# New instruction orders for all five engines of a transformer-layer kernel, and other places for its filler matmuls

## The reference

```python
h = x @ tok_W + position_table                       # (8, 1024, 128)
z = layernorm(h)
q, k, v = z @ Wq + bq, z @ Wk + bk, z @ Wv + bv      # 8 heads of 16
p = softmax((q @ k.T + causal_mask) / 4)             # 1024 x 1024 for each head
h = h + (p @ v) @ Wo + bo
z2 = layernorm(layernorm(h)) * ln_scale + ln_bias
shared = swiglu(z2 @ shared_in.T) @ shared_out.T + b # 256 hidden
hid    = swiglu(z2 @ expert_in.T)                    # 256 hidden, one for all experts
# one of 2 groups by argmax, 2 of its 4 experts by softmax, weights comb (S, 8)
h = h + shared + counts @ expert_bias + sum_e comb[:, e] * (hid @ expert_out[e].T)
```

## Time and profile before

| | |
|---|---|
| median of 3 runs | 1005.61 us (1005.56 to 1009.05) |
| the profiled execution | 1005.95 us, of which 1004.2 us is the span from the first to the last instruction |
| PE busy | 929.9 us, 93% of the span |
| DVE, ACT, POOL busy | 809.5, 595.0, 375.5 us |
| mean granted PE clock | 0.973 of full |

### The profile page before, as it was taken

One profiled execution on the slowest core, in us unless ns is written; L12 is line 12 of the kernel. 1 busy time (PEld: TensorE's weight loads), 2 busy tenths in 40 slices (PEclk: granted clock), 3 DMA queues, 4 the chain that ended last, 5 costly groups with the idle time before them and its releaser, 6 DMA issues.

```text
span 1004.2 us, 17715 instructions
## 1 busy us (share of the span) xinstructions
PE 929.9 (93%) x5672; PEld 548.5 (55%) x5672; DVE 809.5 (81%) x2529; ACT 595.0 (59%) x1365; POOL 375.5 (37%) x526
## 2 busy tenths in 40 slices
PE   6688999999999999999998999999999999999986
PEld 6653454456655646456644656347554655444464
DVE  5688897898779888897979898798978987795363
ACT  4015547665756675756764665666576666666743
POOL 6404322424345243433534253343434152422433
PEclk8789899999989999999999999999999999999999
DMA  4221010200010111110111101110101000100000
GB/s 139 69 67 52 14 33 15 67 30 2 31 59 30 38 31 34 45 48 1 44 35 36 37 17 36 45 54 13 44 20 59 31 12 33 44 2 1 11 11 12
DMA packets 45981, 35.21 MB, mean 35 GB/s; under 512 B 10816, under 2 KB 44608, under 8 KB 45760
## 3 DMA queue, kind: packets, MB, share of 16 engines
q1 hardware_dynamic: 43680, 31.97, 9.8%
q10 hardware_dynamic: 2208, 2.10, 0.6%
HBM read 4.28 MB, written 4.19 MB: 8 GB/s over the span
## 4 chain that ended last, share of the span: by engine, by line
PE 33%; DVE 12%; ACT 3%; issue 3%; POOL 2%; SPq 1%; DMA 1%; ACTq 0%; POOLq 0%; DVEq 0%
PE bank_w L589 5%; PE bank_p L571 5%; PE bank_s L541 4%; PE bank_f L674 3%; PE bank_f L676 3%; PE bank_f L675 3%; DVE mx_far L772 2%; DVE bank_s L776 2%; PE bank_f L475 2%; PE bank_m L640 1%; PE bank_f L477 1%; PE bank_f L476 1%; ACT pt L1043 1%; PE bank_m L604 1%; PE bank_m L614 1%
## 5 line engine op out<-in xcount | busy, mean ns | idle before, releaser
L1043 ACT ACTIVATE pt<-bank_p 128x512 f32<-128x512 f32 (+3 forms) x768 | 342.0, 491 | 188.3 <-PE bank_p L571 158.3
L776 DVE CUSTOM_DVE_ANT_0 bank_s<-bank_s,causal 128x384 f32<-128x384 f32 (+3 forms) x512 | 242.9, 507 | 43.7 <-PE bank_s L541 41.8
L541 PE MATMUL bank_s<-k_stack,q_stack 96*128 96x512 bf16 (+3 forms) x768 | 222.0, 336 | 19.7 <-DVE mx L776 10.5
L571 PE MATMUL bank_p<-q_stack,k_stack 99*128 99x512 bf16 (+3 forms) x768 | 213.3, 334 | 11.2 <-ACT pt L1043 8.0
L772 DVE TENSOR_REDUCE mx_far<-bank_s 128x1 f32<-128x512 f32 x256 | 165.7, 681 | 24.4 <-PE bank_s L541 24.2
L1203 POOL TENSOR_SCALAR_AFFINE_SELECT pt<-pt 128x512 f32<-128x512 f32 x128 | 81.6, 638 | 207.9 <-ACT pt L1043 207.8
L589 PE MATMUL bank_w<-pt,v 128*32 128x512 f32 (+3 forms) x1536 | 153.2, 499 | 3.8 <-POOL pt L1203 1.5
L541 PEld LDWEIGHTS bank_s<-k_stack,q_stack 96*128 96x128 bf16 x768 | 71.8, 100 | 125.1 <-DVE mx L776 44.9
L571 PEld LDWEIGHTS bank_p<-q_stack,k_stack 99*128 99x128 bf16 x768 | 65.5, 99 | 115.7 <-ACT pt L1043 63.8
L674 PE MATMUL bank_f<-wex_h,hid_h 128*128 128x512 f32 x256 | 116.8, 456 | 2.0 <-DVE gate L928 1.3
L1105 ACT ACTIVATE sel<-sel,wsel 128x128 f32<-128x128 f32 x256 | 81.8, 395 | 34.8 <-DVE sel L947 34.3
(11 more groups left out here) (137 smaller groups left out, 1474.1 us busy)
## 6 DMA issues: line engine op xcount, KB each, us to landing
q_stack<-qk_h SPq DMA_DIRECT2D x96, 64.0 KB, 2.6
k_stack<-qk_h SPq DMA_DIRECT2D x84, 64.0 KB, 2.6
q_stack<-qk_m SPq DMA_DIRECT2D x64, 64.0 KB, 2.6
out<-h SPq DMA_DIRECT2D x16, 256.0 KB, 2.3
k_stack<-qk_m SPq DMA_DIRECT2D x56, 64.0 KB, 2.6
q_stack<-qk_l SPq DMA_DIRECT2D x32, 64.0 KB, 2.6
k_stack<-qk_l SPq DMA_DIRECT2D x28, 64.0 KB, 2.6
x_sb<-x_t SPq DMA_DIRECT2D x16, 64.0 KB, 2.1
```

The lines of the kernel that those rows point to most:

```text
L541: nc.tensor.matmul(s_bank[s % 2][:, 0:cols], q_stack[0:STACK, half, hd, t % HT * P:(t % HT + 1) * P], k_stack[0:STACK, hd, key_place(i, ha ...
L571: nc.tensor.matmul(p_bank[p % 2][:, q0:HALF], k_stack[:, hd, key_place(i, kt // HT), kt % HT * P:(kt % HT + 1) * P], q_stack[:, half, hd, ...
L776: nc.vector.tensor_tensor_reduce(src, src, causal[:, HALF - cols:HALF], 1.0, -3.0e38, ALU.add, ALU.max, mx[:, u, col:col + 1]).then_inc(s_ ...
L1043: nc.scalar.activation(pt[:, k % PT_SLOTS, j, q0:HALF], p_bank[p % 2][:, q0:HALF], ACT.Exp, scale=0.25).then_inc(exp_done, 1)
```

## The change

Three things change.

1. All five strings of `ORDER` are new. They hold the same steps: 2224 on PE, 1301 on DVE, 1142 on ACT, 318 on POOL, 123 on SP. A step moves by 9.9 places on PE in the mean, 158 at most; on DVE by 6.8, ACT 4.9, POOL 1.7 (9 at most), SP 1.4 (14 at most). The first 38 steps of PE, through k of half 1 of image 0 and four scores behind it, stand as they did.
2. The fillers of half 1's front in image 0 go (3, 14, 3, 6 and 5), and so do the 7 ahead of v in half 0: 38 fillers. Those ahead of the scores stay.
3. In the last half of the last image 25 fillers are new: 5 ahead of oproj, 14 ahead of z2t, 6 ahead of gates. They write into a score bank, after a wait until all scores of the run are drained.

```diff
-FRONT_FILL = {"emb": (7, 3), "turn1": (8, 14), "q": (8, 3), "k": (7, 6), "v": (7, 5)}
+FRONT_FILL = {"emb": 7, "turn1": 8, "q": 8, "k": 7, "v": 0}
+LAST_FILL = {"oproj": 5, "z2t": 14, "gates": 6}
...
     "pe": (
-        "eeaaaaeessssssassssassssessssstssasssspssassppssssstssppspswssppaspspwsspasppssppswsppspassppwsspassppws"
+        "eeaaaaeessssssassssassssessssstssssasssppasssssssstssssssppspspwssppaspspwssppasppsswssppassppsspassppwp"
...
-        "spwppsappsswpsspssppswppssppswppssappswppsspbpspswppbsspptwppsbsppwpbppsspwasppwspspspspwsspbpspsbspspff"
+        "sfppsshsswwappsswwppssfppssfsstwsswssasssssppseppssptpspspbppsspspsppspssssppsssssbsswwwwbssppsbssppwspp"
...
-        "ssbpfbssppfbssppfssppfssppfssppfssppbsswwwwtppppbwpbppppwppwpppwppppwpphppwppfppfppwppffppwppbfpfppwppf"
-        "ppfwwffbfbfbfbfhffbffbffffbffffffffhffff"
+        "pfsfpsspfspfssppfssppfssppfssppfsppfptpfbwwwwbppppbppwppbwppbppwpphppwppbpwpbppfppfppbwpfppfwppfpfpwpfpp"
+        "fwppffwbfbfbfbffhfbffbffffffffbffffhffff"
...
     "dve": (
-        "ssbsbssbtbbhbbffffbfffffbfbfbbfhbffbbbffbffbffffffhff"
+        "fsstbbbbbhbfbbbbfffffffffbbfbbfbhffbbffbffffbffbffhff"
...
-                    fill(f_bank[0], FRONT_FILL[kind][half])
+                    fill(f_bank[0], FRONT_FILL[kind] if half == 0 else 0)
...
             def post(i, st):
                 kind, half = st[0], st[1]
                 n = half_no(i, half)
+                if n == 2 * B - 1 and kind in LAST_FILL:
+                    pe.wait_ge(s_taken, B * NS)
+                    fill(s_bank[0], LAST_FILL[kind])
```

More of the change, by code:

```diff
@@ L146 @@
[L146 to L160, removed]
@@ new lines @@
+        "sfppsshsswwappsswwppssfppssfsstwsswssasssssppseppssptpspspbppsppspsppspssssppsssssbsswwwwbssppsbssppwspp"
+        "aspspwpbpspsbspsffspptswwffssppapfsfspsfspfssppfssfssbppwbssfbssfssbpspfssbssppfstppwwsspphppsswpbpswpbp"
+        "papfppfppwwppbfpfpeppfpspsfpspswwppssfppsfsppsappfspspfppapspfhpssfssftswwwpssfbppssfbppssfbppssfbppssfp"
+        "psspawwwwppssapspspspwppsstpwppseppswpsbsswppssapsffppssbffppssaffppsswwffppssbpfbppssfbppssfbpspsfbppss"
+        "fhppssfbppsswwwtssppfpspsfssppfssppbssfppsfpspsfpspaswwwpsspffppsstwwppssfppssfappssfppssafppssappsfppss"
@@ new lines @@
+        "bfppsshssfstsfssfsesfsswwwwppssappsspspwppssapspswpsspswppssppsswppssbppswppssppbspwpsptspspwppsbpspswbp"
+        "pssppeppspwppsappswsppswwbppsssbppsffppssaffppssbwwbffppsbsfpfbppssfbppssfppshppssfbsppfssftssppfspbssfs"
+        "appsfssfasswwwwppssfppsfpstpsfpsapsspffppssapspsfppssfpsbswwwwppssfppssfppssfppsshppssfppsstfppssfppssfs"
+        "sfssesswwwwppssbpsspppspspwwbppssppbppsswbppsswpeppssppapspwpspsppwppssptwsbwsssassffppssafpfpssbfpfpssa"
+        "ffppsswwppssbfbppssfbppssfbppssfbppssfpphppssfbssppwwwtssppfsppsbssppfssppfppssawwwppssfppfspspfspstpfss"
@@ new lines @@
+        "papsspwwwppssfppssfppssfpspsappsfppssfppappssfpssbfsshssfstsfssfsesfsswwwwppssappsssspwappsspspwppssbpps"
+        "wppsspbppswpptsswppbspspsbppsswppsappwspspappwppsspbpspswsbspswffppssbpfbfppssbpfpfbpssffbppssfppshppssf"
+        "bppssfsbftssfesswwwwssppbfssppfssppfppassppfsfppsasfppsswwwpptssfpappssfspsfpsspapspsfppssfpspswwwwppssf"
+        "pptssfppsfppsshppssfppssfppssfppssfssfssesswwwwppssbpssppppbppsswwppssappswspsppbspwpsbppsswpptsppappswp"
+        "psppwssppbswspspsaspsffssppbffssppeffssppaffssppwwwsspbpfbssppfbssppfbssppfsshssppftssppfsbssppfsspfsppa"
@@ new lines @@
+        "sfsssbsbsstbsshsssbfbbabfbffssfssfesssfssfassffaashssasssftssfbssbssfssbssbssfabssssssastssesssssssafsfs"
+        "bfsfsbafsfsbabfsfsbabssfbssssfbsbsbhssssfstssssssfssfssfsbsssfsafssbbfsstfbssbssffssassafssasssfsshsssst"
+        "ssfsesassfasssssasssssssssssasssbsssbsstsssssbsbsesbsssassssbsbbfsfsbafsfsbabfsfbsfafssbsbssfbhssssssfts"
+        "ssfbssbsbsabssbssaffssfsstssffssafssfssassfssfssssfsssshssfsstssfssssssfsseassassbssbssssbsbsessbssssast"
+        "ssssssasfsfsafsfbsfbfssbafsfsbassbbssabssfssfbsbsbhsssssftssssbssbssbssbfafssfssfsstssfssfabssfssssfsssf"
@@ L196 @@
+        "pffaapapcccacpppppappppbpabafafpbpcbpcpafaaccfppcpcpcacppppbppppbafafaabpccbpppcfacfpapapcccacpppappppbp"
+        "apabffbpbccpacppcafaafppcpcpcacpppppbpppabaaffapccpcbpcbpafaafpppppccpccppppbppbffppppbccbppfpcpfcbcccbc"
         "ffcccc"
```

58 lines of the change are left out of this document (26 added, 32 removed).

## The result

The changed kernel takes 989.82 us, median of 4 runs (987.45 to 990.75), the kernel before 1006.12 us in the same comparison (4 runs, 1005.56 to 1009.05). The ratio is 0.9829, 95% interval 0.9802 to 0.9855: 16.3 us less, where 3.6 were forecast. The profiled executions have spans of 1004.2 and 988.9 us, 15.3 apart.

A forecast was written before the change was run, and what follows sets the result against it. PE was taken to bound the bulk, DVE the front of image 0. The terms -4.7 - 3.0 + 1.4 - 2.4 + 5.1 + 0 gave -3.6 us, so 1002.0 us, range 992 to 1010.

The forecast's parts named there:

- the sum of the orders: New order strings in bulk and end: four terms, -3.0, +1.4, -2.4 and -1.1 us, together -5.1.
- Weighs in company: PE's bulk: 192 weighs in 116 groups instead of 130, each join saving 0.21 us; -3.0 us, bounds 0 and -5.
- Score runs: PE's bulk: more runs of three to five scores make PE wait for DVE; +1.4 us, bounds 0 and +4.6.
- Long runs of probs at the end: Behind the last score: other work between probs spares PE waits for ACT; -2.4 us, bounds 0 and -3.7.
- The gate ahead of part 2: Run's end, DVE: first gate moved ahead of the last routing's part 2 comes 1.1 us sooner; -1.1 us.
- Rival B: Bulk: new orders halve PE's 16.8 us of waits for maxima and exponentials, giving 993.6 us; chance 0.22.
- Rival D: Image 0's front: without half 1's fillers the clock stays at half from 44 to 70 us, giving 1013.7 us; chance 0.14.
- The front: Image 0: removing fillers ends DVE waits of 3.67, 1.23 and 1.04 us; four fifths taken, -4.7 us, bounds 0 and -5.9.
- The end fillers: Last half of last image: 25 new fillers at 0.25 us each delay PE's queue; +6.2 us, bounds 0 and +6.2.

The follow-up runs named there:

- orders_only: The kernel before with the five new order strings alone, its old front fillers kept and no end fillers: 995.14 us, ratio 0.9882.
- the seams: No front-38 or end fillers: old order until 222, 808 or 918 us, then new (987.22, 991.14, 997.71 us); new until 118 us, then old (1001.13 us).
- old_front_fewer: The kernel before, old orders, with only the 38 fillers of image 0's front removed: 999.64 us, ratio 0.9929.
- new_no_last: The changed kernel without the 25 fillers at the end: 985.95 us, ratio 0.9791 against the kernel before.
- gap_fill_more: The changed kernel without end fillers, plus 31 fillers ahead of image 1's scores 54 to 84 and 21 more in images 0 and 1: 981.31 us.

## Why the prediction was wrong

**The step that failed is the sum of the orders.** Its four terms were -3.0, +1.4, -2.4 and -1.1, and orders_only shows -11.9. They were sized from the drawn lengths of products and from the idle time that the views show, where the waits for maxima and exponentials were 16.8 us and all of PE's idle time 74.3. The gaps between starts were 144.5 us. Sorted by the kinds of the two products on either side, in us with their count, before and orders_only from 78 us on (below zero where a product can follow one of another kind sooner than one of its own):

```
gap between           before        orders_only
score, score       10.4 (x254)     18.6 (x268)
prob, prob          9.4 (x282)      5.7 (x282)
score, prob         9.0 (x203)      4.3 (x193)
score, bank m       5.5 (x101)      0.3 (x90)
prob, weigh         8.5 (x54)       4.7 (x42)
weigh, score       10.3 (x34)       8.0 (x24)
weigh, bank f       4.5 (x14)       2.0 (x4)
weigh, prob        20.7 (x63)      22.8 (x70)
prob, bank f       -2.6 (x70)      -7.8 (x70)
all pairs         119.8           100.1
```

- Weighs in company, -3.0 (0 to -5): gaps at prob to weigh, weigh to score, weigh to bank f fell by 3.8, 2.3 and 2.5, at weigh to prob they rose by 2.1. Net 6.5 in this sorting, so the sign was right and the bound too near: over the 14 joins it is 0.46 us each, where drawn lengths had given 0.21.
- Score runs, +1.4 (0 to +4.6): +8.2 between two scores. By the waits for maxima alone it is less, 11.6 us before and 17.4 in orders_only, but still beyond the bound. The mechanism was right, the size beyond the bound. And the clock falls in the runs of image 1, which costs once more. The count of ten scores also left out image 0, where runs of 7, 6 and 5 stand in place of 5 and 3 from score 27 on.
- Long runs of probs at the end, -2.4 (0 to -3.7): 6.9 us by the gaps, 6.6 by the seams. The mechanism holds for 4.0 of it, from the last score to the last prob, just beyond the bound. The term looked only at 920 to 940 us; the rest comes ahead of the last score, from 860 us on, and stood in no term.
- The gate ahead of part 2, -1.1: -1.2, right.
- What stood in no term: gaps from a score to a prob, from a score to bank m and from a prob to bank f, 15.1 us together. Rival B had said that the bulk fits better, and so it does, but not by its mechanism, which was that 16.8 us of waits are halved: in the changed kernel waits for exponentials fell from 5.2 to 1.5 and those for maxima rose from 11.6 to 17.2. That its 993.6 us was nearest to the measured time is luck.

The sorting tells where the gaps closed, not why; no run isolates these pairs, and which moves of the strings closed them stays open. The seams show only that the gain is spread from 222 to 918 us.

**The half clock** then took 10.5 us of the orders' gain back in the profile of orders_only (31.8 us of it for 21.3), of that 8.9 in image 1 alone. The two profiles are the extremes, 0.960 and 0.973; by the medians of the runs, 0.963 and 0.968, it is about 5 us. Rival D had the front wrong: from 44 to 70 us the clock stays up for 20 of 26 us. A loss came at image 1's scores, which its last sentence names, but from the orders and not from the missing fillers, since orders_only has all of them.

**The front**, -4.7 with the upper bound 5.9, is mis-sized: -7.4 alone and -9.2 under the new orders. DVE's waits of 3.67, 1.23 and 1.04 us are gone and the scores come sooner, as forecast, but by more than the 4 to 5 us forecast: score 31 starts 7.3 us sooner in old_front_fewer and 8.6 in the changed kernel (59.83 for 68.44). Two things were off. The share of four fifths was too low, since those waits turned into progress whole, 5.9 us; and the bound left out that the first score starts 1.1 us sooner (37.62 for 38.71) because its keys do. Together that is 7.0 of the 7.3. Whether the fillers ahead of emb and of v of half 0, costed at nothing, and those ahead of q, in no term, were free, the profiles don't tell: what is left is smaller than the 2 us by which profiles differ where nothing was changed. The clock rose at about 40 us in place of 43, without the fillers that had stood in the queue; in image 1, 31 fillers kept it at 1.00 where it had been at 0.78, 0.83 and 0.68. The Trainium skill, page "TensorE: Matmul & The Clock Gate", section "What's actually happening", says that activity releases the throttled clock. The trace agrees in image 1; in the front the fillers that went were not what released it.

**The end fillers**, +6.2: +5.0 in the old orders, +3.9 in the new. The step is right in kind and too large. A filler follows the last after 0.224 us (3.13 us for 14, from 949.20 to 952.33) and not 0.25, since the 0.25 came from a group's length, which counts the last one's tail; 25 are 5.6. In the changed kernel it is 3.8 us longer from the last score to the last product than in new_no_last. The rest lies in waits that the new orders had brought in, the direction that the prediction named and set at nothing.

**With measured terms**, each taken on the old kernel alone (-7.4, -11.9, +5.0), the sum is -14.3 of the -16.3. The front is worth 1.8 us more under the new orders and the end fillers cost 1.1 less; with intervals some 3 us wide neither difference is certain.

## What to carry over

Read a full engine's room from the distances between starts and not from the bracketed waits: here 144 us of gaps stood beside 74 us of idle time that the profile shows, of which the prediction went by 17. When an order is drawn up, keep independent work back for the stretch in which one kind of product waits for another engine (here 5.5 us of work moved behind the last score, and the gaps there shrank by 4.0). Fillers can pay where PE waits and the clock falls at the wait (31 of them, about -3 us, at the edge of what the intervals tell); ahead of work that waits for nothing they cost nearly their whole length (25 of them, +5.0 in the old orders), and the 25 at the end of the changed kernel are a loss. The changed kernel without its end fillers and with those 31 takes 983.0 us, 0.7% below the changed kernel and 2.4% below the one before; with 21 more 981.3, which can't be told from it.

## What was not expected of the hardware

- A bf16 product of 512 columns is drawn 0.38 to 0.39 us long and the next starts 0.22 us after it, so up to 0.17 us of waiting per product is invisible.
- The clock falls to half here and there in a PE that is over 90% busy, and the places move when something far away is changed: in the kernel before one fall lies at 834.6 us, and with 14 fillers less in the front, at 42 us, there is none there. Between executions of one kernel it differs too: gap_fill_more took 976.8 to 979.6 us at 0.981 to 0.984 and 983.0 to 985.0 at 0.976 to 0.977.
- One of a row of like transfers takes 1.9 us to issue in place of 0.6 in the four kernels that keep ten more fillers ahead of it on TensorE, and the first score starts some 1.1 us later with it. In four of the other ten kernels a later one of the row takes 1.45 to 1.76 us.
